# Attention heads normalised in groups of four instead of eight, and two stages of PSUM evictions moved from VectorE to ScalarE

## The reference

```
scores = q k^T * scale + bias          (masked to the last 512 keys)
p      = exp(scores - m)
out    = (p v) / (sum(p) + exp(sink - m))
x1     = layernorm(x + out @ Wo)
base   = x1 @ weight^T
y      = layernorm(x1 + base + LoRA experts(x1), top 2 of 8 by a router)
```

## Time and profile before

| | |
|---|---|
| median of 2 runs | 2326.25 us (2323.74 to 2328.76) |
| the profiled execution | 2318.29 us |
| span of its slowest core (5) | 2316.6 us |
| spans of the eight cores | 2295.9 to 2316.6 us |
| mean granted TensorE clock | 0.671 to 0.675 |
| TensorE busy (matmul) | 1374.1 us, 59% |
| VectorE busy | 703.8 us, 30% |
| ScalarE busy | 444.7 us, 19% |

### The profile page before, as it was taken

The page is one execution under the profiler, slowest core; times in us unless marked ns, Lnnn a source line. Parts: engine busy times, 40 slices in busy tenths (PEclk is TensorE's granted clock), DMA queues, the critical chain, the costliest instruction groups (busy, mean ns, idle before and its releaser), DMA issues.

```text
span 2316.6 us, 22623 instructions; the slowest of 8 cores (2295.9 to 2316.6 us)
## 1 busy us (share of the span) xinstructions
PE 1374.1 (59%) x8242; PEld 789.0 (34%) x8242; DVE 703.8 (30%) x1348; ACT 444.7 (19%) x838; POOL 188.1 (8%) x208
## 2 busy tenths in 40 slices
PE   3964969989516666555522666655557941378710
PEld 2543855648403322222211223322223421223310
DVE  1000220002234444444433443444441135431232
ACT  0110001110361122222254221122220013100022
POOL 2221112210120000000021000000001100001000
PEclk9987979999755555555555555555558975679955
DMA  6999779996300000000000000000007753427433
GB/s 84 101 112 106 92 100 101 122 127 80 55 1 9 5 5 10 10 10 10 10 9 1 10 9 10 1 9 10 10 1 79 72 105 109 127 22 67 55 129 127
DMA packets 279805, 122.21 MB, mean 53 GB/s; under 512 B 236946, under 2 KB 273938, under 8 KB 275602
## 3 DMA queue, kind: packets, MB, share of 16 engines
q0 software_dynamic: 237168, 74.49, 31.8%
q1 hardware_dynamic: 42530, 46.27, 6.3%
HBM read 174.26 MB, written 20.97 MB: 84 GB/s over the span
## 4 chain that ended last, share of the span: by engine, by line
PE 46%; DVE 17%; DMA 16%; ACT 11%; issue 8%; DVEq 1%; SPq 0%; ACTq 0%; POOL 0%; POOLq 0%
PE psO L650 8%; PE psPT L627 7%; PE psS L449 7%; DVE abf L634 6%; PE psO L511 5%; ACT abf L602 5%; DVE psS L594 5%; PE psS L480 4%; DMA abf<-wv 3%; PE psS L582 3%; PE psO L990 3%; PE psO L765 3%; DMA abf<-wo 3%; DMA abf<-wt 2%; DMA abf<-wq 2%
## 5 line engine op out<-in xcount | busy, mean ns | idle before, releaser
L650 PE MATMUL psO<-abf 128*64 128x128 bf16 x1280 | 182.1, 308 | 191.2 <-DVE abf L634 191.2
L582 PE MATMUL psS<-abf 64*128 64x512 bf16 x256 | 140.7, 587 | 257.8 <-POOL af L379 136.5
L594 DVE SCALAR_TENSOR_TENSOR psS<-psS,af 128x640 f32<-128x640 f32 x256 | 206.7, 831 | 195.5 <-PE psS L590 195.3
L627 PE MATMUL psPT<-abf 128*128 128x128 bf16 x1280 | 182.2, 308 | 103.2 <-DVE abf L621 103.2
L634 DVE COPY abf<-psPT 128x640 bf16<-128x640 bf16 x256 | 125.9, 492 | 326.1 <-PE psPT L627 326.1
L602 ACT ACTIVATE abf<-psS 128x640 bf16<-128x640 f32 x256 | 180.3, 704 | 187.0 <-DVE psS L594 187.0
L650 PEld LDWEIGHTS psO<-abf 128*64 128x64 bf16 x1280 | 128.1, 161 | 251.9 <-issue 251.9
L511 PE MATMUL psO<-abf 128*128 128x256 bf16 x1536 | 175.8, 278 | 33.6 <-DMA abf<-wv 33.5
L519 DVE CAST abf<-psO 128x256 bf16<-128x256 f32 x96 | 40.8, 425 | 497.8 <-PE psO L511 497.8
L449 PE MATMUL psS<-abf 128*128 128x256 bf16 (+1 forms) x1024 | 170.0, 330 | 5.8 <-DMA abf<-wk 4.3
L511 PEld LDWEIGHTS psO<-abf 128*128 128x128 bf16 x1536 | 152.5, 100 | 56.9 <-issue 36.7
(11 more groups left out here) (115 smaller groups left out, 1119.3 us busy)
## 6 DMA issues: line engine op xcount, KB each, us to landing
abf<-wk POOLq DMA_DIRECT2D x32, 512.0 KB, 7.5
abf<-wq POOLq DMA_DIRECT2D x32, 512.0 KB, 9.0
abf<-wv POOLq DMA_DIRECT2D x16, 1024.0 KB, 10.1
abf<-qscr SPq DMA_DIRECT2D x16, 512.0 KB, 4.2
af<-x SPq DMA_DIRECT2D x8, 1024.0 KB, 6.7
abf<-wo POOLq DMA_DIRECT2D x16, 512.0 KB, 6.8
y1scr<-af SPq DMA_DIRECT2D x8, 1024.0 KB, 4.7
af<-y1scr SPq DMA_DIRECT2D x8, 1024.0 KB, 6.7
```

What stands on the lines that cost most here:

```text
L582: t.matmul(psap(psS[sb], 0, [[1, 512]]), lhs, kT[kch][krs:krs + 64, w0:w0 + 512], start=True, stop=(n == 1), tile_position=tp)
L594: tok_t = OP("V", lambda v, sb=sb, hh=hh: v.scalar_tensor_tensor(out=psap(psS[sb], 0, [[1, 640]]), in0=psap(psS[sb], 0, [[1, 640]]), scala ...
L627: tok_tp = OP("T", lambda t, k2=k2, i5=i5, ptb=ptb: t.transpose(psap(psPT[ptb], i5 * 128, [[1, 128]]), pbuf[k2][:, i5 * 128:(i5 + 1) * 128 ...
L650: ins = t.matmul(psap(psO[ob], slot * 128, [[1, 128]], row0=orow, nrows=64), vT[vch][:, h2 * 64:(h2 + 1) * 64], ptsb[ptb][:, i5 * 128:(i5 ...
```

## The change

In attention, the sums, reciprocals, transposes and PV products follow after every fourth head instead of after every eighth, and cover the last four heads. The buffers, the work of each head and the eviction L665 after every eighth head are unchanged. In the Wo product and in the base-weight product, the eviction of each 128x512 result is done by ScalarE (`activation` with Copy) in place of VectorE (`tensor_copy`), at the same place in the program order.

```diff
@@ -606,16 +606,16 @@
-                        if hh % 8 == 7:
-                            h0 = h - 7
-                            gs = slice(h0, h0 + 8)
+                        if hh % 4 == 3:
+                            h0 = h - 3
+                            gs = slice(h0, h0 + 4)
                             tok_c = OP("V", lambda v, gs=gs: v.tensor_add(
                                 denv[:, gs], dsum[:, gs], esnkb[:, gs]),
                                 deps=[tok_e, t_esnk], tick=True)
                             tok_d = OP("V", lambda v, gs=gs: (v.drain(), v.reciprocal(
                                 rdv[:, gs], denv[:, gs]), v.drain())[-1],
                                 deps=[tok_c], tick=True)
-                            for hh2 in range(hh - 7, hh + 1):
+                            for hh2 in range(hh - 3, hh + 1):
...
@@ -769,9 +769,9 @@
-                tok_ev = OP("V", lambda v, o=o, n=n, pb=pb: v.tensor_copy(
+                tok_ev = OP("S", lambda s, o=o, n=n, pb=pb: s.activation(
                     wofm[0:128, o * 1024 + n * 512:o * 1024 + n * 512 + 512],
-                    psap(psO[pb], 0, [[1, 512]])),
+                    psap(psO[pb], 0, [[1, 512]]), ACT.Copy),
                     deps=[last_mm], tick=True)
...
```

## The result

The changed kernel takes 2385.15 us in the median (before, timed beside it: 2323.16). The ratio is 1.0269, 95% interval 1.0248 to 1.0289: 62 us slower, between 58 and 67. In some executions of any kernel here the cores of one die run at a lower granted clock and take some per cent longer; the ratios leave these out, the medians don't. The profiled execution has a span of 2389.6 us on its slowest core, 7.

What follows compares the result with a forecast made beforehand. Attention was taken as bound by a serial chain of engine hand-overs, the Wo and base-weight stretches by TensorE and weight loads. 66.6 - 0.7 - 0.3 = +65.6 us on the 2326.25 median gave 2392, range 2381 to 2402.

Steps and rivals of the forecast that it cites:

- The chain and its cost: Attention: scores phase (first scores to first transposes), then PV phase, never overlapping; 32 splits add 66.6 us.
- The point of 2392: Whole kernel: forecast time, the 2326.25 us median plus 65.6 us, rounded.
- the other stages: Stages outside the two attention stretches: each was to stay within 1 us in the profile after.
- The small instructions: Attention drains: sums and reciprocals on 4 columns instead of 8 save 0 to 1.3 us in all, taken as -0.7.
- The evictions at nothing: Wo and base-weight products: 32 evictions each on ScalarE cost nothing, covered by TensorE's 16 matmuls into the other bank.
- The earlier start of the residual add: After the last eviction in each product: add starts up to 0.3 us sooner, taken as -0.15 each.
- The weight loads: Wo and base-weight loads issued by POOL: no gain from moving the evictions, taken as 0.
- The rival of 19.7 us: Weight loads get quicker by the whole bound, giving 2372; chance 0.05 together with the covered split.
- "what would show it wrong" of 29.9 us: Prediction wrong if TensorE's waits for wo and wt, 29.9 us in all, change by more than a few us.
- The split is covered: Attention rival: fifth head's scores run under the first four's PV phase, about 2326; chance 0.05 together with quicker loads.
- The clock: Attention: TensorE stays at 0.50; the rival, a rise to 2.4 GHz, would give 2264, chance 0.02.

Runs made afterwards that it cites:

- e4_small: Kernel before, groups of eight kept, but sums and reciprocals made four heads at a time, the first four's after the sixth head's score step; ratio 1.0013, attention -1.05 us.
- e2_evict: Kernel before with only the two evictions (Wo and base-weight products) moved to ScalarE, groups of eight kept; ratio 1.001, attention +0.1 us.
- e5_lag: Changed kernel (groups of four, ScalarE evictions) with queues reordered: scores run six heads ahead of transposes and PV product; ratio 0.8412, attention 691.6 us.
- e10_bothfull: e9_kfull with PV also taking 128 columns of V, the eviction keeping 64 rows; correct result; ratio 0.7836, attention 525.0 us.
- e7_notr: e5_lag without the transposes and their copies, attention's result differs; attention 510.8 us, one execution each 1756.4 against 2321.4 us before.
- e8_full: e5_lag with scores over 128 rows and PV over 128 V columns, attention's result differs; attention 522.25 us, one execution each 1788.4 against 2321.4 before.
- e9_kfull: e5_lag with scores contracted over 128 rows, each head's q beside 64 rows of zeros, correct result; ratio 0.8203, attention 630.15 us.
- e3_two: Kernel before with groups of two heads instead of eight, evictions left on VectorE; ratio 1.0893, attention +195.0 us.

## Why the prediction was right

**The chain and its cost.** Predicted: scores phase 7.28 us for four heads with n = 1 and 9.03 with n = 0, measured 7.25 and 9.00; PV phase 8.4, measured 8.39 and 8.37; with n = 1 two groups +1.96 us over one of eight, measured 2 x 15.64 - 29.40 = +1.88. The sum for attention was 66.6 - 0.7 = 65.9 us, measured 64.9. The median moved by 62.0 us, and the ratio's interval is 58 to 67. The point of 2392 lies 7 us over the measured 2385: 3 us because before came out at 2323.16 with more runs, 1 by attention's sum, and 3 in the other stages, which were to stay within 1 us and whose scatter hides a cause if there is one.

The group of the earlier trace rows wasn't a typical one, which did no harm. Over all groups of the two profiled cores the median scores phase with n = 0 is 15.54 us before, not 15.86, and 8.89 after, not 9.03: +2.24 us where +2.20 was predicted. The two deviations cancel, by luck. With the medians for n = 1 (12.60 and 7.25) and for the PV phase (16.80 and 8.38) the sum is 16 x 1.90 + 16 x 2.24 - 32 x 0.04 = 65.0 us, against 64.9 measured.

**The small instructions** were the term that was mis-sized. I took -0.7 us with a bound of -1.3. A reciprocal of four columns takes 178 ns instead of 203, and the sum 163 instead of 168: 64 x 30 ns = -1.9 us, outside the bound. e4_small, with half as many such drains, gained 1.05 us. The 1.2 us between -0.7 and -1.9 account for the 1 us that separates 65.9 from 64.9.

**The evictions at nothing** held: e2_evict, 1.001. ScalarE took 597 ns each, as the earlier trace rows said. TensorE was never to wait for them, but its waits in the Wo product name them for 1.5 us on the slowest core and up to 4.3 on another; with VectorE it was up to 2.8, so little was lost. The earlier start of the residual add is 0.09 us, not 0.15: in the changed kernel it starts 0.79 us after the transposes begin, in the earlier trace rows 0.88.

**The weight loads** stayed at 6.8 us to landing for wo, and TensorE waited 18.2 us for them in the slowest core against 18.6. The rival of 19.7 us didn't occur. The "what would show it wrong" of 29.9 us for both waits was badly chosen: it fell to 22.6 us on the slowest core without any cause in the change, since it was one core's value.

**"The split is covered"** was ruled out by the order in TensorE's queue. That was the right reason: with the order of the queues changed and the same operations (e5_lag), the rival's mechanism does appear and is worth far more than the 62 us.

**The clock** stayed at 0.50 as predicted, but my reason was incomplete. I argued that the busy share doesn't rise. In e5_lag it rose to 95 to 100%, and the clock stayed. So a higher share alone wouldn't have made that rival come true; in these runs it took a change of the matmuls' shape. The rule that sustained activity lifts the rate (the Trainium skill, TensorE: Matmul & The Clock Gate, "What's actually happening") is not enough to tell what happens here: 60.00 busy of 60 us at 0.50 in e5_lag, and 50.00 of 50 us at 0.50 with full matmuls on core 3 of e10_bothfull, speak against taking it for busy time as the profile counts it.

## What to carry to other kernels

A loop that alternates between two phases on in-order queues pays a fill and a drain at each change of phase; read both off the timeline (last piece of work in, first piece of the next phase out), and the cost of another group size is that number less one steady step, times the number of groups added. Smaller groups are a loss by themselves. What they allow is a shorter distance between the phases: the same groups of four, issued six heads behind the scores, turned +2.7% into -16% with the eight probability buffers there are. By the program a group of eight would need more buffers for this; no run tried it. Then look at which engine the removed idle time uncovers, and at the shape of its instructions.

## What the runs showed of the hardware

- TensorE was granted 0.50 throughout attention at 95 to 100% busy when its score matmuls contracted over 64 rows and its PV matmuls filled 64 columns (e5_lag), and at 0.50 without the transposes too (e7_notr). With 128 rows and 128 columns and as many streamed columns it was granted 1.00 at 61% busy (e8_full).
- The same full matmuls were granted 0.50 on core 3 and 1.00 on core 5 of e10_bothfull, both from 700 to 760 of their spans, so the shape alone doesn't fix the clock.
- Half of the stationary rows being zeros didn't keep the clock down (e9_kfull, n = 1: 1.00).
- Beside the levels 0.50 and 1.00 there are stretches at 0.81: 80 us of the projections on core 4 of e3_two with TensorE 100% busy, while core 0 was granted 0.99 over its same window.
- ScalarE evicts 128x512 from f32 to bf16 in 597 ns and VectorE in 692 ns, but an eviction of 64x256 on ScalarE (e10_bothfull) still takes 372 ns, so splitting the psO eviction into 128 pieces raised it from 19.1 to 47.6 us of ScalarE's time.
